# Softmax pieces moved between the steps of a graph-attention edge loop on VectorE, and a SiLU table requested ahead of its use

## The reference

```python
h = relu(layernorm(x))
message = ((h @ w_src + b_src)[src] + (h @ w_dst)[dst]) * edge_weight * radial_mlp(edge_attr_32)
message = message @ w_sep + b_sep                      # per head: 16 for alpha, 16 for value
score   = einsum(smooth_leaky_relu(alpha_part), alpha_dot)
att     = segment_softmax(score, dst)                  # over the edges of one destination
out     = x + (segment_sum(value * att, dst) @ w_proj + b_proj)
```

## Time and profile before

| | |
|---|---|
| time, median of 3 runs | 5095.57 us (5094.09 to 5096.37) |
| the profiled execution's own time | 5094.63 us |
| its span, first to last instruction | 5092.7 us |
| mean granted TensorE clock | 0.973 |
| busy PE / PEld / DVE / ACT / POOL | 4832.5 / 3449.1 / 3848.3 / 2626.1 / 3618.4 us |

### The profile page before, as it was taken

One profiled execution on the slowest core, in us unless ns is written; L12 is line 12 of the kernel. 1 busy time (PEld: TensorE's weight loads), 2 busy tenths in 40 slices (PEclk: granted clock), 3 DMA queues, 4 the chain that ended last, 5 costly groups with the idle time before them and its releaser, 6 DMA issues. The chain is left out here.

```text
span 5092.7 us, 92871 instructions
## 1 busy us (share of the span) xinstructions
PE 4832.5 (95%) x28995; PEld 3449.1 (68%) x28995; DVE 3848.3 (76%) x6981; ACT 2626.1 (52%) x3939; POOL 3618.4 (71%) x3491
## 2 busy tenths in 40 slices
PE   3599999999999999999999999999999999999975
PEld 2456777777776777777677777777777777777764
DVE  6547777777777777777777777777777777777777
ACT  2455555555555555555555555555555555555511
POOL 2377777777777777777777777777777777777716
PEclk9799999999999999999999999999999999999975
DMA  6666666666666666666666666766666666666625
GB/s 188 191 202 200 211 200 212 204 206 207 202 211 202 211 202 206 206 202 211 202 209 205 205 208 199 213 203 207 205 206 208 201 209 205 207 206 206 207 64 157
DMA packets 889681, 1019.24 MB, mean 200 GB/s; under 512 B 161780, under 2 KB 778008, under 8 KB 888863
## 3 DMA queue, kind: packets, MB, share of 16 engines
q1 hardware_dynamic: 758843, 774.32, 47.3%
q0 software_dynamic: 108784, 223.44, 17.6%
q10 hardware_dynamic: 21556, 15.50, 1.2%
HBM read 863.59 MB, written 152.34 MB: 199 GB/s over the span
## 5 line engine op out<-in xcount | busy, mean ns | idle before, releaser
L1056 POOL DMA_INDIRECT gath<-msg_src,idx x3328 | 3475.5, 1044 | 1176.5 <-issue 1030.8
L1245 ACT ACTIVATE sil<-a_ps,ba 128x512 f32<-128x512 f32 x832 | 571.7, 687 | 1648.1 <-PE a_ps L1367 1580.7
L1375 PEld LDWEIGHTS v_ps<-wv,msgT 128*128 128x128 f32 x6656 | 835.5, 191 | 526.2 <-issue 526.2
L1305 PEld LDWEIGHTS rad_ps<-wval,hot 128*128 128x128 f32 x6656 | 911.5, 194 | 79.0 <-DVE wval L1147 35.6
L1305 PE MATMUL rad_ps<-wval,hot 128*128 128x136 f32 x6656 | 929.3, 284 | 32.5 <-DVE wval L1147 31.3
L1375 PE MATMUL v_ps<-wv,msgT 128*128 128x128 f32 x6656 | 924.1, 282 | 0.0
L1367 PE MATMUL a_ps<-msgT,wa 128*128 128x512 f32 x1664 | 890.7, 617 | 30.9 <-DVE msgT L1178 30.9
L1178 DVE TENSOR_TENSOR msgT<-xT_ps,rads 128x512 f32<-128x512 f32 x832 | 572.4, 688 | 354.1 <-PE xT_ps L1348 307.9
L1197 DVE SCALAR_TENSOR_TENSOR sil<-a_ps,sil 128x512 f32<-128x512 f32 x832 | 567.4, 682 | 354.2 <-ACT sil L1245 351.6
L1294 PE MATMUL xT_ps<-hotT,win 128*128 128x256 f32 x3328 | 730.4, 341 | 0.0
L1230 ACT ACTIVATE vals<-v_ps 128x512 f32<-128x512 f32 x832 | 493.2, 593 | 340.4 <-PE v_ps L1375 319.0
(11 more groups left out here) (234 smaller groups left out, 4147.9 us busy)
## 6 DMA issues: line engine op xcount, KB each, us to landing
rows_bc<-edge_rows SPq DMA_DIRECT2D x416, 768.0 KB
win<-msg_dst SPq DMA_DIRECT2D x1664, 128.0 KB
sums<-run SPq DMA_DIRECT2D x416, 272.0 KB
attr<-in_edge_attr_t SPq DMA_DIRECT2D x1664, 32.0 KB
gath<-msg_src,idx POOLq DMA_INDIRECT x3328
msg_dst<-dst_parts SPq DMA_DIRECT2D x98, 128.0 KB, 2.2
pen_g<-pen_rows SPq DMA_DIRECT2D x208, 32.1 KB
mask_g<-mask_rows SPq DMA_DIRECT2D x208, 32.0 KB
```

What stands on the lines that cost most here:

```text
L1056: pool.indirect_dma_start(gath[:, u, s], None, msg_src, bass.IndirectOffsetOnAxis(ap=idx[:, j // 8, at:at + 1], axis=0)).then_inc(s_gath[u ...
L1245: act.activation(sil[:, j % 8], a_ps[:, :], ACT.Silu, bias=ba[:, :]).then_inc(s_sil, 1)
L1305: last = pe.matmul(rad_ps[:, j % 2, AW * i:AW * (i + 1)], lhsT=hot[:, j % 4, s], rhs=wval[:, j % 4, s].rearrange("p h k -> p (h k)"), star ...
L1375: last = pe.matmul(v_ps[:, s * P:(s + 1) * P], lhsT=msgT[:, q, s * P:(s + 1) * P], rhs=wv[:, :], start=True, stop=True)
```

## The change

- `soft` on VectorE: what ran at the end of odd steps goes into even steps. The first addition (L1069) moves from step 1 to step 0; the second pair of ends and the maximum of both scans (L1079, L1081) from step 5 to step 4; the first scan with carries (L1102) from step 9 to step 8. The subtraction of the maximum (L1108), which stood in step 10 behind a scan, becomes the only piece in an odd step: step 11, between `scale_rad` and `sil`.
- In step 14 `mark` now comes ahead of `soft`.
- `weigh` now does one tile. In an odd step one weighted tile comes ahead of `accumulate` and one behind it, where both stood behind it.
- On ScalarE a one-column SiLU into a new tile `spare` follows the two Exps in step 11, so that the table load for SiLU stands there and not in step 12 ahead of `sil`.

```diff
                 def soft(n, j):
-                    if j == 1:
+                    if j == 0:
                         dve.wait_ge(s_sc, 4 * n + 4)
                         ...
                         dve.tensor_scalar(ends[:, 0:G], sel[:, :], fwd[:, TE - 1:TE], None, ALU.mult).then_inc(s_soft, 1)
-                    elif j == 5:
                         dve.wait_ge(s_soft, k + 4)
                         dve.tensor_scalar(ends[:, G:2 * G], sel[:, :], bwd[:, 0:1], None, ALU.mult).then_inc(s_soft, 1)
                         ...
                         dve.tensor_copy(carry[:, 0:1], carry[:, G:G + 1]).then_inc(s_soft, 1)
-                    elif j == 9:
                         dve.wait_ge(s_soft, k + 14)
                         dve.tensor_tensor_scan(bwd[:, :], pen[:, 0:TE], fwd[:, :], carry_in[:, 0:1], ALU.add, ALU.max).then_inc(s_soft, 1)
                     elif j == 10:
                         ...
+                    elif j == 11:
                         dve.wait_ge(s_soft, k + 16)
                         dve.tensor_tensor(shifted[:, :], shifted[:, :], fwd[:, :], ALU.subtract).then_inc(s_soft, 1)
@@ weigh
-                    for n in range(2):
-                        at = 32 * ((j + n) % 4) + H * (j // 4)
-                        last = dve.tensor_tensor(wval[:, u + n], vals[:, slot + n], ...)
-                    last.then_inc(s_wv, 1)
+                    at = 32 * (j % 4) + H * (j // 4)
+                    product = dve.tensor_tensor(wval[:, u], vals[:, slot], ...)
+                    if j % 2:
+                        product.then_inc(s_wv, 1)
@@ step of VectorE
-                    if group(g - 1) and j == 14:
-                        soft(g - 1, j)
                     if j % 2 == 0:
                         if there(t + 2 - LAG):
                             mark(*later(g, j, 2 - LAG))
+                        if group(g - 1) and j == 14:
+                            soft(g - 1, j)
                         if there(t - LAG):
                             accumulate(*later(g, j, -LAG))
                         if group(g - 1) and j != 14:
                             soft(g - 1, j)
                     else:
+                        if there(t + 1 - LAG):
+                            weigh(*later(g, j, 1 - LAG))
                         if there(t - LAG):
                             accumulate(*later(g, j, -LAG))
-                        if there(t + 1 - LAG):
-                            weigh(*later(g, j, 1 - LAG))
+                        if there(t + 2 - LAG):
+                            weigh(*later(g, j, 2 - LAG))
                         if there(t + 1):
                             scale_rad(*later(g, j, 1))
+                    if j == 11 and group(g - 1):
+                        soft(g - 1, j)
                     if there(t):
                         dve.wait_ge(s_sil, t + 1)
                         dve.scalar_tensor_tensor(sil[:, j % 8], a_ps[:, :], 0.25, sil[:, j % 8], ALU.mult, ALU.add).then_inc(s_al, 1)
-                    if j % 2 and group(g - 1):
-                        soft(g - 1, j)
@@ step of ScalarE, j == 11
                         act.activation(drop[:, :], drop[:, :], ACT.Exp).then_inc(s_exp, 1)
+                        act.activation(spare[:, :], row_below[:, :], ACT.Silu)
```

More of the change, by code:

```diff
@@ L887, in gnn_kernel @@
             row_below = tb("row_below", [P, 1])
+            spare = tb("spare", [P, 1])
             rads = tb("rads", [P, 4, TE])
@@ L1144, in weigh @@
                     slot = G * (g % 2) + j
-                    for n in range(2):
-                        at = 32 * ((j + n) % 4) + H * (j // 4)
-                        last = dve.tensor_tensor(wval[:, u + n], vals[:, slot + n],
-                                                 wT[:, :, at:at + H].unsqueeze(3).broadcast_to((P, SUB, H, HV)), ALU.mult)
-                    last.then_inc(s_wv, 1)
+                    at = 32 * (j % 4) + H * (j // 4)
+                    product = dve.tensor_tensor(wval[:, u], vals[:, slot], wT[:, :, at:at + H].unsqueeze(3).broadcast_to((P, SUB, H, HV)), ALU.mult)
+                    if j % 2:
+                        product.then_inc(s_wv, 1)
                 def accumulate(g, j):
```

## The result

The changed kernel takes 5068.6 us (median of 5 runs) against 5095.57 us before, 27.0 less. The ratio is 0.9944, 95% interval 0.993 to 0.9958. One of the five runs took 10372.77 us and is left out of the ratio; it is not explained. The time lies at the lower edge of the stated range, and the gain is 1.9 times the 13.9 us of the sum.

A forecast was written before the change was run, and what follows sets the result against it. PE's queue was taken to set the time in the steady part. Gains of 37.4 us less a loss of 23.5 made 13.9 us less, 5081.7 us for the median, with a range of 5068 to 5096.

The forecast's parts named there:

- the sum: Whole kernel: gains of 28.0 + 2.0 + 7.4 us less a loss of 23.5, so 13.9 us less.
- Part 1, the size of the waits: PE, steady part: waits of 0.55 us in step 10 and 0.04 in step 2 go, gaining 28.0 and 2.0 us.
- Step 10's 0.55 us of waiting go: PE, step 10: moving scan L1102 ahead of step 8's `sil` removes the wait for `msgT`, 51 x 0.55 = 28.0 us.
- Part 1, the order: DVE, steady part: softmax pieces moved to steps 0, 4 and 8 fit into idle time there and delay nothing.
- Part 2, steady part: DVE, odd steps: `msgT` and one weighted tile take 1.25 us against 1.36 to the running sum; zero gain or loss.
- The DRAIN you can't avoid: DVE, odd steps: by this rule, not adopted, each of 8 x 51 would lose 0.05 us, giving a forecast of 5102.
- Part 2, tail: DVE, tail: one weighted tile leaves the path in odd steps, 13 x 0.64 - 0.87 = 7.4 us gained.
- Part 3: ACT, steps 11 and 12: later subtraction and early table load delay the copy; PE waits 0.46 us, 23.5 us lost.

The follow-up runs named there:

- The piece moved alone: Kernel before with only the first softmax addition (L1069) moved from step 1 to step 0: 5084.93 us, ratio 0.9981.
- sums first: Changed kernel without the one-column SiLU, with PE's sum products ahead of the attribute products in odd steps: 5019.66 us, ratio 0.9857.

## Why the prediction was wrong

- **Part 1, the size of the waits: wrong, and the main error.** The sum took a wait on PE as the time until the waiting product starts: 0.55 in step 10, 0.04 in step 2. Measured were 0.66 and 0.15. The step that failed is "Step 10's 0.55 us of waiting go": it took the time to the start of the waiting product for the whole cost and had no term for its weight load, which starts with the product where PE waited and 0.11 ahead where not. The piece moved alone shows it for step 2, all three pieces for both. Over 51 groups that is 51 x 0.22 = 11.2 us of the 12 to 13 missed.
- **Part 1, the order: right.** The pieces are free where they were put: in the kernel with these pieces alone no step grew, and it gains all that the steady part gains.
- **Part 2, steady part: right for this kernel,** by the margin stated, 1.25 against 1.36. Not said was that step 11 lacked that margin before; the edit alone costs 10 us there, and only together with the moved scan L1102 is it free. The rule that the prediction took from the Trainium skill ("VectorE: DVE Perf Modes", The DRAIN you can't avoid), that the next operation waits until the pipe has emptied, would have made the running sum late in all eight odd steps; none was. The same section goes on: "A next op that is not held starts earlier". The prediction left that out, and the 0.60 us from `msgT`, 0.69 long, to its successor fits it.
- **Part 2, tail: mis-sized.** 9.7 for 7.4. The weighted tile off the path is worth at most 9.0. The kernel with the weighted tiles apart alone gained 10.9. That the order of the weighted tile gives most of it is shown: with both tiles behind the sums the tail took 90.89 to 94.42 us in five kernels, with one ahead 79.86 to 85.22 in six. Their means are 9.6 apart, but with such scatter a single pair of executions does not tell 9.7 from 7.4. The granted clock can be a part of it. It fits the pairs (sums in 2.12 or 3.65 us) and two kernels with the same order in the tail, 84.40 at a mean clock of 0.66 and 79.86 at 0.76. It does not fit the kernel with the pieces alone, whose tail took 93.14 at 0.68 against 93.78 at 0.61 before. No run changed the clock alone; its share stays open.
- **Part 3: right in mechanism, off in size.** 0.52 for 0.46, mostly because PE followed the copy by 0.14 and not by 0.06. Cost 26 us, by the kernel without it (26.5 from the steps). The subtraction contributes 51 x 0.46 = 23 us of it with the load in place and nothing without.
- **Balance.** Errors of one sign: +11.2 in the waits, +2.3 in the tail, and +1.2 in head and last stage together, which the sum had at zero; of the other, 51 x 0.06 = 3.1 in step 12. The sum's -13.9 becomes -25.5, and the span's change is -25.9. The 1.2 is scatter: in the eleven kernels here, none of which changes these stages, the head took 253.95 to 256.98 us and the last stage 125.65 to 127.76. That part of the error says nothing of the mechanism. The rest up to 27.0 is the step from the profiled executions to the medians.

## What to carry to other kernels

Price a wait on TensorE by comparing whole steps, start to start, up to a product that is well behind the waiting one: a wait too short to name (0.04 us) cost 0.15, since the weight load lost its cover with it. Before moving an operation ahead of others on an engine, name what stands behind it in that queue and how much time that had in hand; here 1.5 us of cover on ScalarE were spent twice, by a table load and by a later input; the first alone cost 0.06 to 0.09 us a group, the second nothing, both 0.52. An edit that is free in one order may cost its whole gain in another, so test it alone and combined.

## What the runs showed of the hardware

- A product on PE that waits for its data starts its weight load only then: load at 2527.37 with the product, against 0.11 ahead of it without a wait (2608.67 and 2608.78). Where the product changes shape (alpha to radial), this is paid without a wait too: alpha to radial stayed at 0.95 with the running sum done early, where two alpha passes ahead of the value products take 0.86.
- The profile names a releaser of PEld even where PE loses nothing: with sums first, PEld before the radial products is still put down to DVE's running sum (297.5 us in total, 303.3 with both weighted tiles behind), though odd steps are equal with the running sum 0.3 us earlier or later.
- ACT's copy of values was followed by the waiting transposes 0.14 us after its end, in all three kernels where they waited for it (the changed one, the one with the subtraction in step 10, the early table alone).
- A load of ACT's table lasted 1.28 us each time, and the next ACTIVATE, where its input was there, started 1.29 to 1.30 us after the load's start.
